# A software-pipelined hybrid layer on one core: 171 hops in one order for all engines, or 292 parts with a place of their own

## The reference

```
x = x + attn_a(ln(x))     # gated linear attention with level weights (32 heads of 64)
x = x + ffn(ln(x))        # transformer layer: 16-head softmax attention, top-2 of 8 experts
x = x + attn_b(ln(x))     # nine sigmoid gates on shifted values
x = x + ffn(ln(x))        # the same transformer layer again

ln(x)     = (x - mean) / sqrt(var + 1e-5)
attn_a    : z, xBC, dt, dl = x @ W + b;  xBC = silu(causal conv of 4 taps)
            att = (C B^T) * exp(gc_t - gc_s) * lam[level(t, s)];  y = att @ (x * dt) + x * D
            out = rmsnorm(y * silu(z)) @ W_out + b
ffn       : x1 = ln(src + softmax(q k^T / sqrt(8)) v @ Wo);  out = ln(x1 + sum_e w_e * (relu(x1 W1_e) W2_e + b2_e))
attn_b    : out = ln(sum_s roll(v, -s) * sigmoid(x Wg_s)) * gamma + beta
```

## Time and profile before

| | |
|---|---|
| median of 3 runs | 2514.52 us |
| profiled execution | 2524.01 us |
| its span, first to last instruction | 2522.2 us |
| granted TensorE clock, mean | 0.926 |
| busy: PE, DVE, ACT, POOL | 87%, 74%, 57%, 34% |
| chain that ended last: PE, DVE, POOL, ACT | 60%, 22%, 6%, 5% |

### The profile page before, as it was taken

How to read it: one execution, slowest core, us unless ns; L and a number is a source line. 1 busy time by engine, 2 the same in 40 slices (tenths; PEclk the granted TensorE clock), 3 DMA queues, 4 the chain that set the end, 5 groups by cost and what they waited for, 6 DMA issues and landing times.

```text
span 2522.2 us, 47464 instructions
## 1 busy us (share of the span) xinstructions
PE 2191.8 (87%) x16768; PEld 1664.0 (66%) x16768; DVE 1873.0 (74%) x4629; ACT 1429.0 (57%) x2980; POOL 853.2 (34%) x1188
## 2 busy tenths in 40 slices
...
GB/s 140 4 49 7 44 39 50 39 50 20 43 32 39 52 39 52 37 52 4 45 45 39 52 39 50 22 44 29 43 48 39 52 39 48 13 39 40 31 38 5
DMA packets 255194, 100.58 MB, mean 40 GB/s; under 512 B 118552, under 2 KB 253856, under 8 KB 254400
## 3 DMA queue, kind: packets, MB, share of 16 engines
...
## 4 chain that ended last, share of the span: by engine, by line
PE 60%; DVE 22%; POOL 6%; ACT 5%; issue 5%; DMA 2%; SPq 0%; DVEq 0%; POOLq 0%; ACTq 0%
PE psB L802 9%; PE psA L633 7%; DVE work L1119 7%; PE psB L792 7%; PE psA L658 5%; PE psA L572 5%; PE psB L733 4%; DVE nmax L1200 3%; PE psA L609 3%; PE psA L626 2%; POOL O_sb L1405 2%; PE psB L821 2%; PE psA L613 2%; PE psB L698 2%; DVE ff L1277 1%
## 5 line engine op out<-in xcount | busy, mean ns | idle before, releaser
L1119 DVE SCALAR_TENSOR_TENSOR work<-psA,c_conv_w,work 128x255 f32<-128x255 f32 (+2 forms) x864 | 402.0, 479 | 50.8 <-ACT work L876 30.3
L1200 DVE TENSOR_REDUCE nmax<-psB 128x2 f32<-128x512 f32 x512 | 316.0, 680 | 56.3 <-PE psB L700 56.1
L1152 DVE TENSOR_TENSOR att<-att,QK 128x1024 f32<-128x1024 f32 x192 | 245.3, 1304 | 148.1 <-ACT att L903 147.7
L572 PE MATMUL psA<-xnT_a,c_w_in 128*128 128x256 f32 x1088 | 312.6, 414 | 42.7 <-DVE work L1119 42.3
L949 ACT ACTIVATE pt<-psB 128x512 f32<-128x512 f32 x512 | 266.0, 605 | 117.1 <-PE psB L719 117.0
L802 PE MATMUL psB<-c_w,hid 128*128 128x128 f32 x2048 | 278.7, 285 | 10.0 <-ACT pt L949 6.8
L802 PEld LDWEIGHTS psB<-c_w,hid 128*128 128x128 f32 x2048 | 258.7, 198 | 29.2 <-issue 17.8
L792 PE MATMUL psB<-x1T,c_w 128*128 128x256 f32 x1024 | 275.7, 397 | 0.8 <-DVE ff L1277 0.4
L903 ACT ACTIVATE att<-psA 128x512 f32<-128x512 f32 x384 | 204.1, 603 | 126.4 <-PE psA L609 110.0
L1332 POOL TENSOR_SCALAR var_eps<-lnmv 128x2 f32<-128x2 f32 x128 | 40.5, 317 | 691.2 <-DVE lnmv L1010 689.9
L572 PEld LDWEIGHTS psA<-xnT_a,c_w_in 128*128 128x128 f32 x1088 | 210.1, 207 | 96.8 <-DVE work L1119 66.1
...
## 6 DMA issues: line engine op xcount, KB each, us to landing
qk_scr<-qparts SPq DMA_DIRECT2D x192, 192.0 KB, 2.4
...
low<-lvl_scr SPq DMA_DIRECT2D x256, 1.5 KB
...
```

Source lines behind the costliest of these rows:

```text
L572: e.matmul(t[:, 0:T], w_in[:, first + j * P:first + (j + 1) * P], xnT_a[:, :], start=True, stop=True).then_inc(filled[b], 1)
L1119: m = e.scalar_tensor_tensor(out=cv[:, back:], in0=t[:, 0:T - back], scalar=conv_w[:, c, tap:tap + 1], in1=cv[:, back:], op0=ALU.mult, op1 ...
L1152: e.tensor_tensor(att[:, :, :], att[:, :, :], bc(QK[:, kq, :], 1, HG), ALU.mult).then_inc(att_done, 1)
L1200: e.tensor_reduce(nmax[:, i, 2 * h2:2 * h2 + 2], t[:, :].rearrange("p (h k) -> p h k", k=T), AX.X, ALU.max).then_inc(drained[b], 1)
```

## The change

The parts of a hop on different engines get names and places of their own in the table, which now has 292 entries: `conv` (PE), `tap` (ACT), `taps` (DVE); `zgate`, `zact`; `xt`, `xcopy`; `weigh`, `wexp`, `prod` and `sum`, `gated`, `own` (POOL) in the place of `attend`; `es`, `exps`; `smax`, `rowmax`; `up`, `relu`; `down`, `acc`. Each engine still issues what is its own, in the table's order. Tiles, shapes, ring sizes and buffers stay. The table is also cut at another place, which is why `smax0.0` had lag 2 and has lag 1: the samples are as far apart as before. `normalise` uses `scalar_tensor_tensor` with the inverse root as a broadcast tensor, and so does one clamp. The level loads wait for the last `weigh`, not for the last sum.

```diff
 PERIOD = """
-load_x0.0+0 conv0.3+1 silu0.1+1 up0.4+3 silu0.2+1 ep1.3+4 xt0.0+1 conv0.4+1 up0.5+3 lvl0.1+1 silu0.3+1 xt0.1+1
...
+load_x0.0+0 zgate0.7+1 zact0.6+1 zact0.7+1 up1.2+4 maxt0.0+2 mix1.12+3 qk0.0+1 down1.1+4 own0.0+1 relu1.2+4
...
-    if what == "attend":
-        return 0, (2 * (1 + UNITS[k][0]) if k < NU else 0) + (k > 0)
+    if what == "weigh":
+        return 0, 2 * (1 + UNITS[k][0])
+    if what == "sum":
+        return 0, 1
...
                         if n:
-                            e.wait_ge(*full(("attend", 0, n - 1, NU), 0))
+                            e.wait_ge(*full(("weigh", 0, n - 1, NU - 1), 3))
...
-                elif what == "smax":
+                elif what == "rowmax":
                     i = k // 2
                     for j in range(4):
                         h2 = 4 * (k % 2) + j
-                        t, b, u = bank(hop, j)
+                        t, b, u = bank(("smax", lay, n, k), j)
...
             def normalise(y, x, mv, rs):
-                e.tensor_scalar(y[:, 0, :], x[:, 0, :], mv[:, 0, 0:1], rs[:, 0:1], ALU.subtract, ALU.mult).then_inc(*own.step())
-                return e.tensor_scalar(y[:, 1, :], x[:, 1, :], mv[:, 1, 0:1], rs[:, 1:2], ALU.subtract, ALU.mult)
+                for i in range(NT):
+                    m = e.scalar_tensor_tensor(out=y[:, i, :], in0=x[:, i, :], scalar=mv[:, i, 0:1], in1=bc(rs[:, i], 1, HID),
+                                               op0=ALU.subtract, op1=ALU.mult)
...
-                    e.tensor_scalar(ln_dt[:, :, :], SPL[:, :, 0:H], 1e-37, None, ALU.max).then_inc(dt_in, 1)
+                    e.scalar_tensor_tensor(out=ln_dt[:, :, :], in0=SPL[:, :, 0:H], scalar=1e-37, in1=SPL[:, :, 0:H],
+                                           op0=ALU.max, op1=ALU.max).then_inc(dt_in, 1)
```

More of the change, by code:

```diff
@@ new lines @@
+tail0.1+2 smax1.1+3 rowmax1.1+3 tail0.2+2 ssq0.0+1 smax1.2+3 rowmax1.2+3 tail0.3+2 ssq0.1+1 ssq0.2+1 ssq0.3+1
+smax1.3+3 outp0.0+1 rowmax1.3+3 maxt1.0+3 down1.6+4 gates0.4+0 outp0.1+1 tail0.4+2 acc1.6+4 gates0.5+0
+gates0.6+0 v1.0+3 outp0.2+1 es1.0+3 exps1.0+3 place0.0+0 fn0.0+1 tail0.5+2 conv0.0+0 up0.0+2 ep1.0+3 es1.1+3
+relu0.0+2 up1.7+4 exps1.1+3 relu1.7+4 conv0.1+0 fn0.1+1 tap0.0+0 tail0.6+2 ep1.1+3 experts0.0+2 lvl0.0+0 es1.2+3
+exps1.2+3 q0.0+1 taps0.0+0 down1.7+4 acc1.7+4 experts1.2+4 experts0.1+2 ep1.2+3 up0.1+2 tap0.1+0 es1.3+3
@@ L126, in order @@
+up1.0+3 relu1.0+3 taps0.8+0 up1.1+3 relu1.1+3 experts1.0+3 mix1.6+2 mix1.7+2 mix1.8+2 down1.0+3 xcopy0.6+0
+zgate0.4+0 experts1.1+3 acc1.0+3 zact0.4+0 mix1.9+2 mix1.10+2 zgate0.5+0 smax0.3+1 zact0.5+0 rowmax0.3+1
+zgate0.6+0 silu0.8+0 mix1.11+2
+"""
+SILU_SET = ("silu", "zact", "mix")
+EXP_SET = {"gates": (2, 3, 4), "wexp": range(NU), "exps": range(NH // 4), "tail": (5,), "outp": (1,)}
 def order():
@@ L899, in _ @@
                         for half in range(2):
-                            t, b, u = bank(hop, 2 * s + half)
+                            t, b, u = bank(("weigh", 0, n, k), 2 * s + half)
                             c = half * 64
@@ L1110, in _ @@
                     e.tensor_copy(high_sel[2][0:3 * H, :], tb[0:3 * H, 0:P]).then_inc(drained[b], 1)
[L1111 removed]
+                elif what == "taps":
                     pair = conv_pair(k - 1)
                     for j, c in enumerate(conv_tiles(k)):
[L1114 removed]
+                        t, b, u = bank(("conv", 0, n, k), j)
                         cv = pair[:, j, :]
```

203 lines of the change are left out of this document (100 added, 103 removed).

## The result

The changed kernel takes 2416.42 us (median of 4 runs, 2413.47 to 2420.85), against 2515.68 (2509.86 to 2528.47) for the kernel before on the same chip: a ratio of 0.960, with a 95% interval of 0.956 to 0.964. The forecast was 2470. The direction was right and the time lies in the range, but the gain is 99 us where 43 were forecast. In the later sets of runs, with 9 to 23 runs of the kernel before in each, its median was 2522 to 2525 us. The 99 us, against a median of four, are therefore more likely a little low than high.

What follows compares the result with a forecast made beforehand. PE was taken to bound the turn, busy 132.1 of 143.4 us. Terms -3.0 - 1.5 + 2.3 - 1.0 + 0.1 = -3.1 us a turn, over 14 turns -43 us, gave 2514.5 - 43 = 2471, say 2470; range 2405 to 2555.

Steps and rivals of the forecast that it cites:

- the hole ahead of the mix: PE's single 2.21 us wait for DVE's `src` before the mix's transposes; claimed to fall to about 1 us.
- part 3: End of the attention: new PE waits at the last sum and around `smax1`, +2.3 us a turn (0 to +3.6).
- part 1: Stretch up to the mix: idle time stays 5 to 6 us, half clock partly goes, -3.0 us a turn (bound 5.1).
- the count of 14 turns: Of 16 turns' worth of samples, 14 counted as gaining, since the ramps gain little: -43 us over the run.
- What bounds: Full turn: PE bounds it, busy 132.1 of 143.4 us; an order can remove idle time, half-clock loss and DVE-bound losses.
- Part 2: At `es1.1`: PE's wait for DVE's copy of `O_sb` goes, -1.5 us a turn (0 to -1.5).
- Part 4: Small PE waits, among them the norms ahead of q: -1.0 us a turn (0 to -3.0).
- Parts 5 and 6: Scaling's new form: 350 against 340 ns, +0.1 us a turn; level loads waiting for the last `weigh`: 0.
- (a): Rival: the waits only move and the clock near the mix still falls, -0.1 us a turn, 2513 us; chance 0.18.
- (b): Rival: attention's end becomes a second DVE-bound stretch, slower, 2586 us or 2544 without a second low clock; chance 0.28.
- (c): Rival: nearly all half-clock loss and waits go, -9.6 us a turn, 2380 us; chance 0.10.
- the signs: Turn about 140 us, PEclk 1.00, L818 under 1.5 us, L726 near 0, new 1 to 3 us wait at L634 or L706.

Runs made afterwards that it cites:

- hole: Changed kernel with smax0.1 and conv0.8 moved back behind the mix's transposes on PE: 2445.27 us, ratio 0.9691 to the kernel before.
- hole_fill: Kernel of `hole` plus four discarded matmuls on PE ahead of the wait for the mix's `src`: 2429.49 us, ratio 0.9619 to the kernel before.
- warm_half: Kernel before plus discarded matmuls in PE's idle pieces ahead of the mix, every engine's order unchanged: 2513.76 us, ratio 0.9963.
- old_place1: Changed kernel with the order of before, except smax0.1 and conv0.8 ahead of the mix's transposes on PE: 2516.9 us, ratio 0.997 to the kernel before.
- ts_norm: Changed kernel with the old `tensor_scalar` form back in the norms and the clamp: 2412.76 us, ratio 0.9561 to the kernel before.

## Why the prediction was right and wrong

The mechanism was right: PE's clock and its idle time are what a turn loses, and the hole ahead of the mix goes. Sizes were wrong. The term of the sum that failed most is part 3, +2.3 us a turn for waits at the end of the attention, where none was measured there: the last product was ready 2.6 us behind the last weights, not 4.8. With it fail part 1, -3.0 for the clock where -4.8 was measured, and the count of 14 turns where the gain is that of 18.4.

**What bounds.** Right. PE's busy and idle time make up the turn, and the gain lies in the clock and the idle time: 4.8 and 1.2 us of the 6.0.

**Part 1, the stretch up to the mix.** The two sums of DVE's excess (4.0 and 3.9) foretold that PE's idle time there would stay, and it did: 6.0 us before, 6.2 after. That two sums of rounded hop prices came so close is in part luck. The long wait for the transposes went from 38.7 us to 10.9 (7.3 for a maximum, 3.6 once for `src`). The clock no longer falls, and that was worth more than the 3.0 us a turn that I took: 4.8 by PE's busy time, near the bound of 5.1. That bound came from one turn at a mean clock of 0.96; the ten turns were at 0.95, so it was a little low. I had discounted for a low clock that follows the total idle time, and it doesn't. `hole` and `hole_fill` show that the long piece matters, `warm_half` that it isn't all: there it was filled and the clock fell later, after new waits. What the changed order has, and no filling gave in the order of before, is a mix whose groups find their banks free: they wait for no maximum, where they wait for 14.6 us in `warm_half` and 14.8 in `old_place1`.

**Part 2, `es1.1`.** The wait for `O_sb` at `es1.1` is gone, as forecast. But v now stands right ahead of `es1.0` on PE, whose last bank waits until DVE has taken `V`: 8.9 us in the run. So 1.5 us a turn became 0.6.

**Part 3, the end of the attention.** This is the step that failed most: +2.3 forecast, none measured at the last sum and a tenth or two of a us at `smax1.2`. PE's timeline from the last weights to the last sum shows no wait:

```profile
1588.48 0.38 PE L621 MATMUL psA<-low,low_sel 125*128 125x256 bf16 x2
1588.70 0.27 PE L706 MATMUL psB<-k_stack,q_stack 72*128 72x256 bf16 x1
...
1589.58 0.60 PE L634 MATMUL psA<-c_ident,own 128*128 128x128 f32 x4
1590.11 1.97 PE L641 MATMUL psA<-att,X 128*64 128x128 f32 x32
1592.01 0.66 PE L634 MATMUL psA<-c_ident,own 128*128 128x128 f32 x4
```

DVE, same stretch, then ACT:

```profile
1587.40 1.23 DVE L1164 TENSOR_TENSOR att<-att,QK 128x1024 f32<-128x1024 f32 x1 [0.19 <-ACT att L911]
1588.54 0.60 DVE L1289 SCALAR_TENSOR_TENSOR ff<-psB,w_e,ff 128x128 f32<-128x128 f32 x2
1589.06 2.36 DVE L1164 TENSOR_TENSOR att<-att,QK 128x1024 f32<-128x1024 f32 x2
1591.34 2.47 DVE L1212 TENSOR_REDUCE nmax<-psB 128x2 f32<-128x512 f32 x4
```

```profile
1584.32 0.60 ACT L911 ACTIVATE att<-psA 128x512 f32<-128x512 f32 x1 [1.06 <-PE psA L617]
...
1587.87 2.07 ACT L911 ACTIVATE att<-psA 128x512 f32<-128x512 f32 x4 [0.57 <-PE psA L617]
```

The last weights end at 1588.86, the last product at 1591.42: 2.6 us later and not 4.8. ACT began the first of its two last hops 4.5 us ahead of that end (1584.32) where I took 2.3, and was through 1.1 us behind it (1589.94) where my figures make 2.5. PE reaches the last sum at 1592.01, after 3.2 us (3.5 forecast). The two sums ahead of the last weights do wait for `att` (0.26 and 0.59 us in this turn; 13.4 in all, 2.1 before), a term that I hadn't.

**Part 4.** The norms ahead of q fell from 23.6 to 6.4 us, 1.1 a turn, as forecast. But new waits took back more than that: a tanh ahead of `up1.1` and `ff` at `tail1.1`, 19.6 and 19.1 us. So idle time as a whole fell by 1.2 a turn only, though the waits of parts 1, 2 and 4 all shrank. With the measured 4.8 in place of 3.0 and nothing in place of +2.3 my own sum would be -7.2; the 1.2 too much are new waits that I didn't name, those for `att` among them.

**Parts 5 and 6.** Right. The new form takes 344 ns, 350 forecast and 340 before; the change of form is within what can be told. The rule of the Trainium skill in "VectorE: DVE Perf Modes" (section on the perf-mode tier table), by which float32 `tensor_scalar` from SBUF runs at twice the rate of an operation on two tensors, isn't borne out with two pointers here: 340 and 344 ns, and `ts_norm` is not clearly faster. SP's wait stayed.

**The count of turns.** This step failed too. I counted 14 turns and let the ramps gain little. The filling and the emptying turns gained some 24 us each, beside 60 in the ten full ones and 3 at the start: 110.6/6.0 = 18.4 turns' worth. They run at a lower clock than the full ones (0.91 and 0.86 before) and with PE idle for a larger share, so there was more to win, not less. One full turn is among those counted as filling.

By the forecast's own terms, for the 110.6 us of the profiled executions: 14 x 3.1 = 43; the missing 2.9 a turn make 41 of the rest, the 4.4 uncounted turns 26.

**Rivals.** (a) has PE's idle time right and the clock wrong. (b) fell with part 3. (c), given 0.10, is nearest in its reason (the clock at full, the waits at both places gone) and was 36 us off in time, less than the 54 of the forecast. Of the signs, the turn, PEclk, L818 and L726 came as named; the new wait of 1 to 3 us at L634 or L706 didn't: L634 has 0.8 us a turn, and L706 9.1 us in all, at `smax0.1`.

**Open.** What in the sequence of idle pieces brings the clock down isn't settled: one long piece does it in `hole`; in `warm_half` short ones do, of 1.02 us at most and 3.3 us in 20; in the changed kernel 6.2 us in 24 don't, with pieces up to 1.45 us. So neither the sum nor the longest piece decides by itself. Nor is it shown which engine's order brings the rest of the gain: no run moves one engine's list alone, beyond these single places on PE.
